# A routed expert block on one Trainium2 core: the prologue's work laid out anew over the engines, and constant matmuls behind TensorE's later routing steps

## The reference

```python
x = x + jnp.tanh(g_xattn[0]) * _L0_xattn_ref(ctx_1024, ctx_1024, _layernorm(x, axis=-1), L0_xattn_Wk, L0_xattn_Wv, ...)
x = x + jnp.tanh(g_ffn[0]) * _L0_ffn_ref(_layernorm(x, axis=-1), L0_ffn_gate_w, L0_ffn_w1, L0_ffn_b1, L0_ffn_w2, L0_ffn_b2)
...
kp = jnp.einsum('bsd,ed->bse', k, Wk)
vp = jnp.einsum('bsd,ed->bse', v, Wv) + bv
qp = jnp.einsum('bsd,ed->bse', q, Wq) + bq
scores = jnp.einsum('bqd,bkd->bqk', qp, kp) * scale
probs = jax.nn.softmax(scores, axis=-1)
ctx = jnp.einsum('bqk,bkd->bqd', probs, vp)
return jnp.einsum('bqd,ed->bqe', ctx, Wo) + bo
...
probs = jax.nn.softmax(logits, axis=-1)
topk_probs, topk_idx = jax.lax.top_k(probs, TOP_K)
oh = jax.nn.one_hot(topk_idx, NUM_EXPERTS, dtype=x.dtype)
h = jnp.einsum('bsd,fed,bske->bskf', x, w1, oh)
h = h + jnp.take(b1, topk_idx, axis=0)
h = jax.nn.gelu(h)
y = jnp.einsum('bskf,def,bske->bskd', h, w2, oh)
y = y + jnp.take(b2, topk_idx, axis=0)
out = jnp.sum(y * topk_probs[..., None], axis=-2)
```

## Time and profile before

| what | us |
|---|---|
| median of 3 runs (lowest, highest) | 100.55 (99.87, 100.81) |
| the profiled execution: time | 99.57 |
| its span in the trace | 97.8 |
| busy: PE, DVE, ACT, POOL | 78.7, 66.9, 52.4, 45.3 |

### The profile page before, as it was taken

The page is one execution under the profiler, slowest core; times in us unless marked ns, Lnnn a source line. Parts: engine busy times, 40 slices in busy tenths (PEclk is TensorE's granted clock), DMA queues, the critical chain, the costliest instruction groups (busy, mean ns, idle before and its releaser), DMA issues.

```text
span 97.8 us, 2758 instructions
## 1 busy us (share of the span) xinstructions
PE 78.7 (80%) x789; PEld 64.6 (66%) x789; DVE 66.9 (68%) x290; ACT 52.4 (54%) x158; POOL 45.3 (46%) x69
## 2 busy tenths in 40 slices
PE   4987787675786401995899999999999999999940
PEld 1374455463574300331579999999999999999930
DVE  2178899999989787089765566568978665324980
ACT  4166489998984604200296576576575674742000
POOL 6965700017787777710001764564654655205600
PEclk9999999998555555559999999999999999999999
DMA  2999999940111119303442454000111001067015
GB/s 21 311 396 424 415 389 331 330 139 27 54 58 54 54 54 236 94 27 89 113 101 64 121 154 112 30 26 30 32 34 54 12 27 54 26 214 219 3 50 164
DMA packets 11630, 12.58 MB, mean 129 GB/s; under 512 B 1363, under 2 KB 10599, under 8 KB 11360
## 3 DMA queue, kind: packets, MB, share of 16 engines
q1 hardware_dynamic: 9808, 9.74, 31.1%
q0 software_dynamic: 1088, 2.05, 6.5%
q10 hardware_dynamic: 720, 0.62, 2.5%
HBM read 8.18 MB, written 4.42 MB: 129 GB/s over the span
## 4 chain that ended last, share of the span: by engine, by line
PE 43%; DVE 25%; POOL 12%; issue 9%; DMA 4%; ACT 2%; DVEq 1%; POOLq 0%
PE bank L724 21%; POOL dispatched L362 10%; PE bank L710 5%; PE bank L712 5%; PE bank L711 5%; DMA wp<-in_wpack 4%; DVE w_lo L924 4%; PE bank L699 3%; DVE xn L792 2%; POOL rstd L398 2%; DVE out_sb L1027 1%; DVE x L850 1%; PE bank L721 1%; DVE s_sub L838 1%; DVE stats L799 1%
## 5 line engine op out<-in xcount | busy, mean ns | idle before, releaser
L547 ACT ACTIVATE hid<-bank,wp 128x128 f32<-128x128 f32 x92 | 26.3, 368 | 22.4 <-PE bank L712 22.2
L426 POOL DMA_INDIRECT results<-y_sb,in_rows x18 | 17.9, 994 | 24.0 <-DVE y_sb L1001 12.2
L724 PE MATMUL bank<-w_sb,hid 128*128 x184 | 25.6, 282 | 0.0
L362 POOL DMA_INDIRECT dispatched<-rows,slot x16 | 15.7, 983 | 14.6 <-DVE slot L919 10.6
L724 PEld LDWEIGHTS bank<-w_sb,hid 128*128 128x128 f32 x184 | 22.4, 192 | 0.0
L710 PE MATMUL bank<-xs_t,w_hi 128*128 128x128 f16 x92 | 17.1, 220 | 0.1
L711 PE MATMUL bank<-xs_t,w_hi 128*128 128x128 f16 x92 | 17.1, 219 | 0.0
L712 PE MATMUL bank<-xs_t,w_lo 128*128 128x128 f16 x92 | 17.1, 219 | 0.0
L556 PE MATMUL bank<-ones 128*128 128x512 bf16 x26 | 10.4, 584 | 5.9 <-DVE tile_rows L975 4.6
L995 DVE COPY xs_t<-bank 128x256 f16<-128x256 f16 x23 | 6.7, 291 | 6.6 <-PE bank L699 6.5
L556 PEld LDWEIGHTS bank<-ones 128*128 128x128 bf16 x26 | 3.4, 136 | 11.6 <-issue 9.3
(11 more groups left out here) (158 smaller groups left out, 143.2 us busy)
## 6 DMA issues: line engine op xcount, KB each, us to landing
w_sb<-in_w SPq DMA_DIRECT2D x2, 2048.0 KB, 11.8
in_rows<-dispatched SPq DMA_DIRECT2D x23, 65.0 KB, 1.9
results<-zeros SPq DMA_DIRECT2D x1, 1024.0 KB, 11.1
res<-results SPq DMA_DIRECT2D x4, 256.0 KB, 3.7
ctx_sb<-in_ctx_t SPq DMA_DIRECT2D x1, 512.0 KB, 5.6
out<-out_sb SPq DMA_DIRECT2D x4, 128.0 KB, 2.0
wp<-in_wpack ACTq DMA_DIRECT2D x1, 342.0 KB, 3.7
dispatched<-pad_rows SPq DMA_DIRECT2D x5, 65.0 KB, 3.6
```

Of the source, the lines that this page charges most:

```text
L362: pool.indirect_dma_start(rows_dram, bass.IndirectOffsetOnAxis(ap=slot[:, t, k:k + 1], axis=0), rows[:, t, k, :], None).then_inc(sent_late ...
L426: pool.indirect_dma_start(results_dram, bass.IndirectOffsetOnAxis(ap=in_rows[:].bitcast(U32)[:, t, TARGET:TARGET + 1], axis=0), y_sb[:, t, ...
L547: mm = act.activation(hid[:, t % HIDS, b, :], hid_ps[t % HID_PS][:, b * P:(b + 1) * P], ACT.Gelu_apprx_tanh, bias=b1[:, bass.ds(experts[t] ...
L724: mm = pe.matmul(to, hid[:, t % HIDS, b, :], w2_sb[:, bass.ds(e, 1), b * P:(b + 1) * P], start=False, stop=b == BLOCKS - 1)
```

## The change

The first layer norm goes by the four groups. Its statistics and the normalising of groups 0 and 1 are DVE's, that of groups 2 and 3 is ACT's (NORMALISE_ACT, with a bias that DVE makes in NORM_BIAS), and all of it stands in the table, whose numbers are new. The transfers of x go in four parts, with the context's between the second and the third. The fused query weights have a copy of their own (`query_ok`), ahead of the fused values' (FUSE_VALUES, COPY_FUSED). POOL takes `x_bias`, the casts of `numbers`, and the inverse root of the second norm for group 0 (ROOT_POOL); `constants` moves into the table too. EXP_LOGITS writes the sum of the exponents itself. All four W1_HIGH stand late in the table, and two quarters of W1_LOW are in it. From QUERIES of the last group on, each PE step is followed by two constant matmuls (HELD). The first two expert tiles are turned by PE in FP32 straight from `in_rows`; ACT writes the high part and DVE the low one.

```diff
-PIECES = [(0, 2), (2, 4), (4, 8)]
+POOL_ROOTS, ACT_NORMS = 1, 2
...
-    MAXIMUM: [11.3, 12.7, 16.6, 23.9],
-    FILL: [21.0, 24.6, 32.4, 36.7],
+    MAXIMUM: {0: 10.7, 1: 13.2, 2: 19.5, 3: 24.5},
+    FILL: {0: 18.9, 1: 23.9, 2: 28.9, 3: 34.7},
...
+PE_STEPS = (NORM_T, QUERIES, SCORES, PROBS_T, ATTEND, X1_T, ROUTE, RANKS, VALUES)
+HELD = 2
+W1_LOW_EARLY = 2
...
+            load_x(0)
+            load_x(1)
             sp.dma_start(ctx_sb[:], ctx_t).then_inc(ld_ctx, 16)
+            load_x(2)
+            load_x(3)
...
+            def biased_input(g):
+                pool.wait_ge(ld_x[g], 16)
+                if g == 0:
+                    pool.wait_ge(bias_ok, 1)
+                pool.tensor_tensor(x_bias[:, group(g), :], x_sb[:, group(g), :], out_bias[:, None, :].to_broadcast((P, SIZES[g], P)),
+                                   ALU.add).then_inc(xbias_ok, 1)
...
+            def normalise(g):
+                act.wait_ge(norm_bias_ok, g - ACT_NORMS + 1)
+                for t in tiles_of(g):
+                    act.activation(xn[:, t, :], x_sb[:, t, :], ACT.Identity, bias=norm_bias[:, t:t + 1],
+                                   scale=rstd[:, t:t + 1]).then_inc(xn_act_ok, 1)
...
-                    m = act.activation(exps[:, t, :], shifted[:, t, :], ACT.Exp, scale=rstd2[:, t:t + 1])
+                    m = act.activation(exps[:, t, :], shifted[:, t, :], ACT.Exp, scale=rstd2[:, t:t + 1], accum_out=exp_sum[:, t:t + 1])
...
+            for t in range(LAG):
+                act.wait_ge(xs_in_ps, t + 1)
+                act.activation(xs_t[:, t, 0, :], xs_ps[t % 2][:, 0:P], ACT.Copy).then_inc(head_ok, 1)
...
+            turned = ORDER.index((QUERIES, GROUPS - 1))
+            for at, (step, g) in enumerate(ORDER):
...
+                if at >= turned and step in PE_STEPS:
+                    keep_clock(xnt_bank[:, :], HELD)
...
+            def turn_first(t):
+
+                pe.wait_ge(loaded[t], 16)
+                pe.transpose(xs_ps[t % 2][:, 0:P], in_f[:, t, 0:P], ident[:]).then_inc(xs_in_ps, 1)
...
             for t in range(LAG):
-                turn_rows(t)
+                turn_first(t)
...
+            def norm_biases(g):
+                v.wait_ge(rstd_ok, g + 1)
+                v.scalar_tensor_tensor(norm_bias[:, group(g)], meanvar[:, group(g), 0], -1.0, rstd[:, group(g)],
+                                       ALU.mult, ALU.mult).then_inc(norm_bias_ok, 1)
...
+            def first_low(t):
+
+                v.wait_ge(head_ok, t + 1)
+                v.tensor_tensor(xs_t[:, t, 1, :], xs_ps[t % 2][:, 0:P], xs_t[:, t, 0, :], ALU.subtract).then_inc(xs_ok, 1)
...
                     for u in range(LAG):
-                        split_rows(u)
-                    for u in range(LAG):
-                        copy_rows(u)
+                        first_low(u)
                     bias_low()
                     split_rows(LAG)
```

More of the change, by code:

```diff
@@ L94 @@
[L94 to L100 removed]
+    NORM_STATS: {0: 4.0, 1: 5.1, 2: 6.6, 3: 7.4},
+    NORM_BIAS: {2: 8.8, 3: 9.6},
+    NORMALISE: {0: 6.0, 1: 9.0},
+    NORMALISE_ACT: {2: 10.6, 3: 13.1},
+    OUT_BIAS: {0: 4.8},
+    FUSE_VALUES: {0: 5.8},
+    COPY_FUSED: {0: 7.4},
@@ L184, in gated_block @@
         half_var = sb("half_var", [P, TILES], F32)
+        norm_bias = sb("norm_bias", [P, TILES], F32)
         near_square = sb("near_square", [P, TILES], F32)
@@ L398, in root @@
                 return pool.tensor_tensor(to, with_eps, power, ALU.pow)
-            for i, (a, b) in enumerate(PIECES):
-                h = slice(a, b)
-                pool.wait_ge(var_ok, i + 1)
-                root(rstd[:, h], var_eps[:, h], meanvar[:, h, 1], minus_half[:, h]).then_inc(rstd_ok, 1)
+            for g in range(GROUPS):
+                pool.wait_ge(var_ok, g + 1)
+                root(rstd[:, group(g)], var_eps[:, group(g)], meanvar[:, group(g), 1], minus_half[:, group(g)]).then_inc(rstd_ok, 1)
@@ L418, in _ @@
+            for step, g in ORDER:
+                if step == CONSTANTS:
+                    constants()
+                elif step == NUMBERS:
+                    numbers()
+                elif step == X_BIAS:
+                    biased_input(g)
+                elif step == ROOT_POOL:
+                    rstd_of(g)
+                elif step == SEND_A:
                     send(pool, g, STARTS[g])
@@ L944, in _ @@
                     fill_rows_of(g)
+            v.wait_ge(numbers_set, 5)
+            then(v.tensor_tensor(lane[:, 0:1], lane_at[:], lane_i[:], ALU.add))
             v.wait_ge(count_ps, 1)
```

267 lines of the change are left out of this document (142 added, 125 removed).

## The result

| | median us (lowest to highest) | executions |
|---|---|---|
| before | 100.68 (99.87 to 100.92) | 4 |
| after | 104.75 (103.87 to 105.72) | 4 |

The changed kernel takes 1.0328 of the time before, 95% interval 1.025 to 1.0407: slower by 3.3%, outside the predicted range. Ratios here compare executions in the quicker of the chip's two states alone and medians take all executions, so the two can differ by about 1%: by the medians it is 4.0%. The profiled execution of after took 105.46 (span 103.7), about 1.5 above the two shortest, so its sum is read for places rather than for its last microsecond.

What follows compares the result with a forecast made beforehand. The prediction took the way to the first slot, then POOL's scatter pace, to bound the kernel up to 42 us. Of 1.9 us won in front, 0.3 go to DVE and 1.0 to PE's block: 100.55 - 0.6 = 99.95, range 98.3 to 101.2.

Steps and rivals of the forecast that it cites:

- The way to the first slot: Prologue up to group 0's slot: slot ends at about 19.5, first scatter starts at 19.8 in place of 21.69.
- The third rival: POOL's new work blocks DVE: slot 3 about 0.9 later, experts start at 47.5, time 100.9; chance 0.12.
- The later slots: From slot 0 to slot 3: 15.0 of DVE work plus 0.9 of waiting, slot 3 at 35.4 (before 34.99).
- the way to the logits of group 2: PE from about 22.1: seven steps and five constant pairs at 0.43 each, logits at 26.5, DVE there at 25.6.
- The end of the scatters: Last scatter over at 40.4, 1.6 earlier; loads issued 1.69 after it, at 42.1, and landing at 44.0.
- What is late next: PE's block of 17 constant matmuls, from 39.3, frees PE at 45.5, 1.5 after the tiles; first hidden matmul 46.6.
- The second: Clock falls in the prologue after a PE wait from 8.8 to 10.4: slot 3 2.5 later, 102.5; chance 0.11.
- the first rival: PE's constant block is short, 3.6 to 4.5 us, so the loads bound: experts start at 45.1, 98.5; chance 0.27.

Runs made afterwards that it cites:

- the run with the padding early and the pairs: Changed kernel, constant pairs kept, with pad_from ahead of the last group's fill and ScalarE's four padding transfers ahead of its last W1_HIGH: 102.15 us, ratio 1.021.
- holes filled: Changed kernel, pairs kept, plus six constant matmuls ahead of group 1's NORM_T and five ahead of group 0's RANKS: 101.59 us, ratio 1.014.
- Without pairs and with the padding late: Changed kernel with HELD 0 instead of 2, padding transfers left in place, run twice: 101.63 us, ratio 1.019, and 101.19 us, ratio 1.003.
- The run with group 1 early: Changed kernel without pairs, padding issued earlier, NORMALISE of group 1 at 7.0 instead of 9.0, POOL's numbers at 13.0: 99.47 us, ratio 0.995.

## Why the prediction was wrong, by its own steps

Two terms of the sum failed: the full clock for the pairs behind TensorE's steps between slot 0 and slot 3, and the fixed 1.69 us from the last scatter to the loads.

**The way to the first slot** failed by the clock for the most part. The maximum came at 11.37 (11.1 predicted). Then the queries of group 1 took 1.22, where they took 0.70 at full clock in the run with the padding early and the pairs, and `rden` stood at 14.98 instead of 14.0. In that other run `rden` was at 13.91 and slot 0 ended at 19.83 (19.5 predicted). Two smaller terms were off: POOL's root took 0.72 and DVE's `nbias` behind it 0.68, beside a POOL `x_bias` that started at 17.69, where the later ones take 0.16; and the sum of the exponents costs ACT 0.19 for each tile. The third rival named this collision; it cost about 0.5 once, not 0.9.

**The later slots** failed by the pairs at half clock. I had 15.9 from slot 0 to slot 3, with a pair at 0.43. It was 18.34 with the pairs at 0.86 and the clock at 0.50 from 21 to 27.5, 15.87 with the pairs and the holes filled, and 15.73 without pairs at 0.55: it takes both, the pairs and the low clock. What is wrong is the sentence that took the full clock for the way to the logits of group 2: I had read 1.00 up to 23.5 off one execution of the kernel before, whose PE had no hole of that size there, and carried it over to an order that makes one. (The seven steps of that sentence are six, as its list has them; the 26.5 is right for six.)

**The end of the scatters** failed in "the loads were issued 1.69 after the last scatter". I took a number that contains a landing time for a constant. The scatter lands 2.3 after its start, 1.3 of the 1.69, and the rest is SP's waits; and in the table of the last four scatters the landing grows with the padding beside it. Pulling the scatters in by 1.6 while slot 3 stays puts the padding on top of the last ones: +1.6, as large as the whole gain. (In after it is slot 3 that came late; the scatters end 5.3 behind it, where it was 7.0 before.) This was in no rival. Moving the padding alone is worth 1.2% of the time in the changed kernel and 1.2 to 2.8% without the pairs, all across chips, and 2.2% in the kernel before, on one chip, where a part is the clock behind the late start.

**What is late next** was right in kind and wrong in size. I had PE's constant block free at 45.5 and 1.5 behind the tiles. In after it ran from 43.10 for 6.25, and the first tile landed at 49.63: 0.33 of waiting for the load, none for the block. Without pairs and with the padding late the first turning waited 0.87 for its load in one profile and met the end of the block in the other. With the loads at 43.7 to 44.3 the block can be in the way: from the loads to the first hidden matmul it is then 3.46 to 3.64 in four runs, and 3.16 and 3.29 in two, where others have 3.06 to 3.17, so the block costs up to 0.6. The run with group 1 early comes closest to my picture: block from 39.31, loads at 42.49. There the block was through at 44.6 and not at 45.5, after 5.30 us and not 6.2, since the clock came back sooner, and it kept the first tile, landed at 44.31, waiting for 0.1. So the block's length was mis-sized too; it ran for 5.3 to 6.8 in the profiles of the changed order.

**The rivals.** The second is what happened: a hole in PE's work that the new order makes, a fall, pairs at 0.86. The mechanism was right, chance (0.11) and size were not, and the place only in part: the hole that it names, ahead of group 1's turning, opens the first fall, and the pairs stand in the second. It priced slot 3 at +2.5 over my 35.4, 37.9; it was 39.24, with a second hole ahead of the ranks of group 0, a second fall behind it and the pairs in that fall, and I had counted on dense work bringing the clock back soon. And the landing adds 1.6 that it lacked. Its argument against, "the same steps held 1.00 before", was the weak one: the steps were the same, the gap between them was not. The rule of the Trainium skill that I had set beside the first rival (TensorE: Matmul & The Clock Gate, Why this matters for your kernels) is that the clock falls back in an idle gap between bursts. The trace agrees in direction only: the clock fell behind the holes of 0.96 and 1.15 at 10.22 and 19.50, but these are much shorter than the gaps that the Trainium skill warns of there, and behind holes of 0.97 and 1.26 at the first place it stayed at 1.00 in two other profiles. I had written that no row showed the gap of this change, but had worked out that gap myself, 8.8 to 10.4.

The start of the experts is 3.8 later in the profile, the profiled time 5.9. The remaining 2.1 lie behind the start, where the span less the start is 50.7 before, 50.6 to 52.1 in the profiles of the variants and 52.8 in after. They are not in the head: PE's work from the first hidden matmul to its last one takes 47.19 in after and 46.85 before. The rest is in the final sums, where POOL waited 2.45 for its last `res` in after and 0.72 before, and in the last outgoing transfers: from the start to the first `out` it is 48.1 against 46.9, from there to the end 4.7 against 3.8. Whether the change has a part in that was not settled; the other profile of the same kernel has 51.8 behind the start.

## What to carry to other kernels

When an order is changed, list the idle gaps that the new order leaves on TensorE ahead of the steps that wait for it, and price these steps, and every constant matmul put between them, at half clock as well as at full. Constants that are to hold a clock belong into the gap; behind each step they are queued work, and at half clock they cost twice. In this prologue they never paid: with both holes filled and the clock at 1.00 the kernel still stood at 1.014, without pairs at 1.003 and 1.019. And when a chain is pulled in, ask which transfers keep their place: a delay from issue to issue, read off a trace, holds a landing time that changes with what flies beside it.

## What the runs showed of the hardware

- An indirect scatter of 128 rows lands mostly 2.3 us after its start alone, and up to 5.7 (holes filled; 5.3 in the table) beside eight plain transfers of 65 KB to the same tensor; these landed in 3.2 us (median) before and 3.6 in after.
- The same program had the clock fall in one execution and hold in another: 0.50 and 0.80 from 21 to 27 with the same PE program up to there, slot 3 2.4 us apart, 1.1 of them from slot 0.
- POOL's first indirect transfer started 2.07 and 2.08 us behind its last cast in the two runs in which the casts and a wait for them stood right ahead of it, with its slot ready 0.94 before.
- Eleven constant matmuls more made the kernel with pairs faster, 1.014 against 1.033 of the kernel before, with a mean granted clock of 0.933 to 0.955 against 0.880 to 0.926.
- A clock at 0.55 from 21 to 27 us cost the slots nothing that shows when no constants stood in PE's queue: 15.73 us from slot 0 to slot 3, and 15.87 at full clock with constants.
